# 32-head self-attention on one core: the batch loop written out, values and row sums in one product, one inversion for two tiles, sums added on GpSimd, the output product split over two steps

## What is computed

```python
q, k, v = split(x @ Wqkv)                 # 32 query heads of 16, 8 key heads of 16, 8 value heads of 16
s = causal(q_h @ k_g.T * 16 ** -0.5)      # 256 x 256 for each of 32 heads
p = exp(s - rowmax(s)); o_h = (p @ v_g) / rowsum(p)
o = o_even - lam * o_odd                  # differential attention, lam from four vectors
y = (o * (1 - LAMBDA_INIT)) @ w @ Wproj   # done as two products, output_1 and output_2
out = layernorm(x + y)
```

## Time and profile before

| | |
|---|---|
| median of 3 runs | 2690.73 us (2687.52 to 2690.77) |
| profiled execution | 2702.13 us, span 2700.4 us |
| busy in the span | PE 2359.3 us, DVE 1950.1, ACT 1423.8, POOL 1619.5 |
| self-attention stage | the first 680 us of the span |
| `self_neg_max`, two maxima a slot, L1503 and L1504 | 256 each, 422 and 682 ns |
| exponentials of the stage, L1366 | 256, 813 ns |
| masks of the stage, L1582 | 256, 659 ns |

### The profile page before, as it was taken

How to read it: one execution, slowest core, us unless ns; L and a number is a source line. 1 busy time by engine, 2 the same in 40 slices (tenths; PEclk the granted TensorE clock), 3 DMA queues, 4 the chain that set the end, 5 groups by cost and what they waited for, 6 DMA issues and landing times. The chain is left out here.

```text
span 2700.4 us, 64172 instructions
## 1 busy us (share of the span) xinstructions
PE 2359.3 (87%) x23480; PEld 1977.8 (73%) x23480; DVE 1950.1 (72%) x3223; ACT 1423.8 (53%) x2223; POOL 1619.5 (60%) x1937
## 2 busy tenths in 40 slices
PE   5999999998698986988999984888995899987998
PEld 5777777776566656988999983777775667656998
DVE  3677776776488973536888866999984488875776
ACT  2566656665366653324556654566562466653333
POOL 3677666764467752175666656777664488863443
PEclk9899999999699987999999997999996799988999
DMA  8566565651798951135666653011001888841111
GB/s 206 132 154 163 144 140 144 159 129 33 215 223 220 230 131 36 41 114 194 224 219 222 226 173 112 28 44 48 21 13 56 222 211 224 215 119 41 49 57 51
DMA packets 227284, 363.44 MB, mean 135 GB/s; under 512 B 51968, under 2 KB 156416, under 8 KB 219520
## 3 DMA queue, kind: packets, MB, share of 16 engines
q1 hardware_dynamic: 207392, 281.32, 39.3%
q0 software_dynamic: 17376, 78.13, 8.5%
q10 hardware_dynamic: 2304, 1.05, 0.2%
HBM read 231.72 MB, written 133.69 MB: 135 GB/s over the span
## 5 line engine op out<-in xcount | busy, mean ns | idle before, releaser
L1366 ACT ACTIVATE self_probs<-self_score_ps 128x768 f32<-128x768 f32 x256 | 208.2, 813 | 199.2 <-PE self_score_ps L1268 197.3
L1582 POOL TENSOR_SCALAR_AFFINE_SELECT self_probs<-self_probs 128x512 f32<-128x512 f32 x256 | 168.5, 659 | 174.5 <-ACT self_probs L1366 174.5
L1503 DVE TENSOR_REDUCE self_neg_max<-self_max_ps 128x2 f32<-128x256 f32 x256 | 108.1, 422 | 178.5 <-PE self_max_ps L88 178.5
L647 ACT ACTIVATE cross_probs<-cross_score_ps 128x1024 f32<-128x1024 f32 x128 | 131.2, 1025 | 101.6 <-PE cross_score_ps L545 100.1
L745 DVE TENSOR_REDUCE cross_neg_max<-cross_max_ps 128x4 f32<-128x1024 f32 x128 | 154.7, 1212 | 39.9 <-PE cross_max_ps L524 39.8
L1504 DVE TENSOR_REDUCE self_neg_max<-self_max_ps 128x2 f32<-128x512 f32 x256 | 174.5, 682 | 0.0
L2294 POOL TENSOR_TENSOR moee_h_lo<-moee_h,moee_h_hi 128x512 fp32r<-128x512 f32 x78 | 112.5, 1443 | 92.1 <-ACT moee_h_hi L2031 91.3
L739 DVE TENSOR_REDUCE causal_block_max<-causal_max_ps 128x6 f32<-128x768 f32 x128 | 120.9, 946 | 56.1 <-PE causal_max_ps L88 55.6
L3589 POOL TENSOR_TENSOR ffn_g_lo<-ffn_g_full,ffn_g_hi 128x512 fp32r<-128x512 f32 x64 | 82.2, 1284 | 129.5 <-ACT ffn_g_hi L3475 116.5
L2031 ACT ACTIVATE moee_h_hi<-moee_h 128x512 fp32r<-128x512 f32 x110 | 69.6, 633 | 167.6 <-DVE moee_h L2197 159.4
L647 ACT ACTIVATE causal_probs<-causal_score_ps 128x768 f32<-128x768 f32 x128 | 103.6, 810 | 98.9 <-PE causal_score_ps L545 98.8
(11 more groups left out here) (507 smaller groups left out, 9493.7 us busy)
## 6 DMA issues: line engine op xcount, KB each, us to landing
self_q<-self_q_split SPq DMA_DIRECT2D x48, 512.0 KB, 3.6
self_q_raw<-self_q SPq DMA_DIRECT2D x32, 768.0 KB, 8.1
cross_stacks<-cross_qk SPq DMA_DIRECT2D x64, 384.0 KB, 6.5
causal_stacks<-causal_qk SPq DMA_DIRECT2D x64, 384.0 KB, 6.5
moe_y_tiles<-lasting_y_out SPq DMA_DIRECT2D x55, 256.0 KB
mid<-lasting_y_out SPq DMA_DIRECT2D x48, 256.0 KB, 2.2
x_tiles<-zeros SPq DMA_DIRECT2D x16, 624.0 KB, 5.0
moee_xT<-x_tiles SPq DMA_DIRECT2D x39, 256.0 KB
```

Of the source, the lines that this page charges most:

```text
L647: nc.scalar.activation(probs[i // 2][:, a, :, lo:], score_ps[:, :, lo:], ACT.Exp, scale=HD ** -0.5).then_inc(prob_ready, 1)
L1366: nc.scalar.activation(probs[g % 4][:, a, :, P:], score_ps[:, :, P:], ACT.Exp, scale=HD ** -0.5).then_inc(prob_ready, 1)
L1503: dve.tensor_reduce(neg_max[:, tile, :, c, 0:1], bank[:, :, 0:P], AX.X, ALU.max, negate=True)
L1582: pool.affine_select(diagonal, diagonal, [[0, 2], [0, 2], [1, P]], ALU.is_ge, zero, base=0, channel_multiplier=-1).then_inc(prob_masked, 1)
```

## The change

`run` writes out all twenty steps; the hardware loop of the stage is gone. `weighted` has 8 products where it had 16: `v_pad` holds a column of ones in the unused half, and each group writes its own half of `out_ps`. ScalarE makes a masked copy with the halves exchanged (`cross_weighted`), VectorE adds the rest (`merge`), and this frees the bank. GpSimd adds the sums of two tiles (`add_sums`) and VectorE inverts once for two tiles; a shuffle spreads the inverse (`scale`). The two maxima of a slot become one over three blocks and a join for each tile.

Work is moved as well: `transpose_x`, `x_hi` and `x_lo` of a batch from slot 0 of a step to slots 12 and 13 of the step before; `output_1` from slots 12 and 14 to 14 and slot 0 of the next step; `y_hi` and `y_lo` to slots 0 and 1; `part_o` to slots 6, 7, 14 and 15; `finish_rows` from slot 7 to 11; ScalarE's `sort_q` is cut in halves, in slots 3, 4, 12 and 13. The transfer of `ones` is gone, for all stages.

```diff
 def mask_half(pe, bank, identb, mask, ab, step):
-    diagonal = bank.rearrange("p (j t) -> p j t", t=P)[:, 0::3, first:]
+    diagonal = bank[:, 0:3 * P].rearrange("p (j t) -> p j t", t=P)[:, 0::2, first:]
...
-        run = lambda eng, body: batches(eng, body, -3, B, 6, 5)
+        def run(eng, body):
+            for t in range(-3, B + 1):
+                body(Step(0, t))
...
             def output_1(st, half):
-                if not st.has(-1):
+                if half == 0 and not st.has(-1):
                     pe.wait_ge(w_lo_ready, 2)
                 if half == 0:
-                    if st.has(3):
+                    if st.has(4):
+                        pe.wait_ge(xlo_ready, st.done(4))
+                    elif st.has(3):
                         pe.wait_ge(v_kept, st.done(3))
                     elif st.has(-1):
                         pe.wait_ge(r_ready, st.done(-1))
-                n = st.at(0) * TILES + 2 * half + 2
+                n = st.at(-half) * TILES + 2 * half + 2
                 pe.wait_ge(ohi_ready, n)
                 pe.wait_ge(olo_ready, n)
...
                 if par == 0 and (tile or st.has(d - 1)):
-                    pe.wait_ge(comb_ready, st.at(d) * TILES + tile)
-                for part in range(4):
-                    k = part % 2
-
+                    pe.wait_ge(merged_ready, st.at(d) * TILES + tile)
+                for k in range(QT):
                     first_q = P if k == 1 else 0
                     cols = slice((1 - k) * S + first_q, (2 - k) * S)
                     for quad in range(4):
                         rows = slice(32 * quad, 32 * quad + 32)
-                        if part < 2:
-                            lhs = v_pad[p][:, 2 * (4 * (quad // 2) + tile) + k, par, :, :].rearrange("p a e -> p (a e)")
-                            out0 = 0
-                        else:
-                            lhs, out0 = ones[:, par, :], S
-                        last = pe.matmul(out_ps[rows, out0 + first_q:out0 + S], lhs,
+                        lhs = v_pad[p][:, 2 * (4 * (quad // 2) + tile) + k, par, :, :].rearrange("p a e -> p (a e)")
+                        last = pe.matmul(out_ps[rows, par * S + first_q:(par + 1) * S], lhs,
                                          probs[g % 4][:, quad % 2, quad // 2, cols],
-                                         start=(par == 0 and part == 0),
-                                         stop=(par == 1 and part == 3), skip_group_check=True)
+                                         start=k == 0, stop=k == QT - 1, skip_group_check=True)
...
+            def join_max(st, tile):
+                dve.wait_ge(max_kept, st.at(1) * PAIRS + 4 * tile + 4)
+                if st.has(0):
                     dve.wait_ge(maxT_done, st.at(0) * TILES + tile + 1)
+                dve.tensor_tensor(neg_max[:, tile], block_max[:, :, :, 0:2], block_max[:, :, :, 0::2],
+                                  ALU.min).then_inc(max_joined, 1)
+
+            def merge(st, d, tile):
+
+                n, b = st.at(d) * TILES + tile, tile % 2
+                dve.wait_ge(crossed_ready, n + 1)
+                if tile >= 2 or st.has(d - 1):
+                    dve.wait_ge(o_ready, n - 1)
+                dve.scalar_tensor_tensor(merged[b][:], out_ps[:].rearrange("p (a s) -> p a s", s=S),
+                                         halves[:, 0:1], crossed[b][:], ALU.mult, ALU.add).then_inc(merged_ready, 1)
+
+            def invert(st, d, half):
+                dve.wait_ge(sums_ready, st.at(d) * 2 + half + 1)
+                dve.reciprocal(inv_sum, sums).then_inc(inv_ready, 1)
+
             def normalize(st, d, tile):
 
                 n, b = st.at(d) * TILES + tile, tile % 2
-                dve.wait_ge(comb_ready, n + 1)
-                dve.reciprocal(inv_sum[:, b, :], comb[b][:, 1, :]).then_inc(inv_ready, 1)
-                dve.wait_ge(inv_ready, n + 1)
+                dve.wait_ge(inv_ready, st.at(d) * 2 + tile // 2 + 1)
+                if tile or st.has(d - 1):
+                    dve.wait_ge(o_ready, n)
+                dve.stream_shuffle(scale[:], inv_sum, [HD + b] * HD + [b] * HD).then_inc(scale_ready, 1)
+                dve.wait_ge(scale_ready, n + 1)
                 if tile >= 2 or st.has(d - 1):
                     dve.wait_ge(olo_ready, n - 1)
-                dve.tensor_tensor(o_full[:, b, :], comb[b][:, 0, :], inv_sum[:, b, :],
+                dve.tensor_tensor(o_full[:, b, :], merged[b][:, 0, :], scale[:],
                                   ALU.mult).then_inc(o_ready, 1)
...
+            def add_sums(st, d, half):
+                n = st.at(d) * 2 + half
+                pool.wait_ge(merged_ready, 2 * n + 2)
+                pool.tensor_tensor(sums, merged[0][:, 1, :], merged[1][:, 1, :], ALU.add).then_inc(sums_ready, 1)
```

173 lines of the change are left out of this document (99 added, 74 removed).

## The result

The changed kernel took 2715.06 us, median of four runs (2708.81 to 2722.76). The kernel before took 2689.63 in the same comparison. The ratio is 1.010, with a 95% interval of 1.0075 to 1.0126: 1.0% slower, where the prediction said 1.3% faster. The profiled execution took 2722.76 us, with a span of 2721.0.

A forecast was written before the change was run, and what follows sets the result against it. TensorE was taken to bound a full step, VectorE next. Savings of 15.3 + 3 + 7.6 + 4.5 + 2 - 2 gave 30 us, taken as 34 for overlapping waits: 2656 us, range 2620 to 2684.

The forecast's parts named there:

- The loop: Self stage: writing out steps 3 to 10 removes three back edges, which cost 15.3 us together.
- A group: Products with values and sums on TensorE: each group shrinks from 1.43 us to 0.79, eight groups a step, 5.1 us.
- The wait in slot 7: TensorE waits about 1.8 us a step for VectorE's merge of tile 2 before writing `out_ps` for tile 3.
- The wait in slot 14: TensorE's first output product waits for VectorE's `x_lo`: 1.9 to 3.4 us, taken as 2.7.
- The wait in slot 0: TensorE's second output product waits 0.8 us for `o_lo` of tile 3, made by GpSimd in slot 15.
- the lock: Slot 13: if GpSimd's `sort_k` starts first, VectorE's product with the scale stands until it ends; slot 14 then waits 3.4 us.
- the sum of a full step: Self stage: 31.1 us of TensorE work plus waits of 1.8, 2.7, 0.8 and 0.3 gives 36.7, as before.
- Steps 13 and 14 are set by VectorE: End of the self stage: VectorE's 26.93 us, about 1.5 and its own waits make 30; 3.8 us saved each.
- The head: Start of the self stage: step 0 saves 4.5 us, step -1 saves 2, eight more memsets cost 0.5.
- TensorE alone decides: Rival: waits of slots 7, 14 and 0 are hidden, full step 31.1 us, kernel 2594 us; chance 0.10.
- The lock strikes in every step: Rival: slot 14 costs 3.4 us each time, 8 us more in all, 2665 us; chance 0.18.
- the lock and a clock that falls: Rival: after slot 14's 3.4 us wait TensorE runs slow, 2 us more a step, 2688 us, no change; chance 0.14.

The follow-up runs named there:

- the loop alone: The kernel before with only the self stage's hardware loop written out: 0.9956 of before, 12 us less.
- the wait filled: The changed kernel with 44 unneeded products of 128 bf16 columns on TensorE in slot 14's wait, ahead of the first output product: 1.0037 of before.
- the kernel with the sort in slot 12: The changed kernel with GpSimd's sorting of k moved from slot 13 to slot 12: 1.0002 of before.
- The kernel without the sums: The kernel before with the loop written out and the products with `ones` left out for all batches but the first: 0.9843 of before.
- the kernel with ten products in slot 7: The changed kernel with `x_lo` made before slot 13's normalize, k's sort in slot 12, ten unneeded products ahead of slot 7's merge wait: 0.9918 of before.
- `x_lo` first: The changed kernel with VectorE making `x_lo` ahead of the normalizing product in slot 13: 0.9982 of before.
- two products to a slot: The changed kernel with `x_lo` before slot 13's normalize, k's sort in slot 12, two unneeded products in every slot of steps 13 and 14: 0.9969 of before.

## Why the prediction was wrong

The account of the self stage, in us against the kernel before, from the traces (where a step starts, and where the last product of the stage does; by another row as the start of a step the parts shift by up to 0.4):

| part | forecast | measured | missed by |
|---|---|---|---|
| head and steps -1, 0 | -6 | +0.9 | 7 |
| steps 1 to 11, and the loop's edges | -15.3 | 26.9 - 15.3 = +11.6 | 27 |
| step 12 | -3 | -1.5 | 1.5 |
| steps 13 and 14 | -7.6 | +13.0 | 21 |
| step 15 and the tail | +1.5 | +6.3 | 5 |
| sum | -30 | +30 | 61 |

The terms of the prediction add up to 30, and it then took 34 for small waits that overlap. The measured column is 30.3, and the profiled execution is 20.6 us above that of before; the other 10 came back between the experts and the causal stage, which the change leaves alone. The time from the first `moee_y_ps` to the first product of the causal stage is 1040 us in the trace of before, 1030 in that of after, and 1023 to 1047 in those of the experiments, so I put it down to no cause.

**What held.** The loop: 15.3 forecast, 14.5 in the trace of the loop alone. A group: 0.79 us. The wait in slot 7: 1.8 forecast; 0.98 for the merge and 0.43 for the maxima in a full step, 1.83 in steps 13 and 14. The wait in slot 14: 2.7 taken of 1.9 to 3.4; it is 2.67, and 0.59 for the exponential ahead of it, near the upper end. The wait in slot 0: 0.8 forecast, at most 0.7. The walk over VectorE's slots was sound, and so was the lock: the page "SBUF — State Buffer" of the Trainium skill, section "SBUF: two separate sides", says that whichever of the two engines starts first holds it, and the sort does so in every step. TensorE's work in a full step was put at 31.1 and is 31.6 (34.27 with the wait filled, less 2.63 for the 44 products), VectorE's at about 30 and is 29.9.

**The step that failed** is the sum of a full step: "31.1 + 1.8 + 2.7 + 0.8 + 0.3 = 36.7". It adds waits as if TensorE came out of them as fast as it went in, and so puts the clock's term at nothing. At the full clock the step would be 37.3, as the filled wait shows, 0.6 above the forecast; the clock makes it 38.7, and 39.2 on average over the eleven, since the low stretch is longer in some (a step of 44.1 us among them). The row for it was in hand: an edge of the loop cost 5.1 us where the wait was 3.16. Busy time by stretch of the kernel before, behind the three edges, has the clock too:

```profile
276.90:280.10 3.20, 3.20 (x42) 1.77 (x38) 1.78 (x4) 1.04 (x2) 3.12 (x5) 0.50 0.57 136
355.40:358.60 3.20, 3.20 (x38) 1.64 (x36) 1.62 (x3) 0.74 (x2) 3.11 (x4) 0.50 0.77 166
430.50:437.10 6.60, 5.83 (x49) 4.03 (x53) 2.58 (x5) 2.49 (x4) 3.07 (x5) 0.50 0.20 41
```

The prediction used the row only for a rival, at 2 us a step, which is the right size, and gave it 0.14, because the wait was to be 2.7 and not 3.4. A wait of 2.67 us is long enough, and one of 1.3 still brings it in ten steps of eleven (the kernel with the sort in slot 12).

**The second failure** is "Steps 13 and 14 are set by VectorE ... 30". That took the saved TensorE work of steps that have no projections as a gain. The trace of before warned of it, if less plainly: TensorE was idle for 2.5 of 33.77 us there already, where a full step had 0.5. With the groups' 5.1 us gone as well, the granted clock is 0.74. The kernel without the sums loses 5.4 of the 13.0 us, so that much comes with the shrunken groups alone; no run parts the other 7.6 among the new and moved operations. Nor was 30 us reached where the clock came back. The nearest row is step 14 of the kernel with ten products in slot 7, which takes 34.1 us at a clock of 0.95, against 39.8 at 0.70 in the changed kernel. By it some 6 us a step are the clock's, and some 4 are waits that the 30 left out (an estimate from these two rows).

**The head** was missed by 7 us. Step 0 was to take 32.3 (36.76 less 4.5), and took 39.6 at a clock of 0.77. With `x_lo` first it took 31.4 at 1.00. Busy time by stretch of step 0, changed kernel and `x_lo` first:

```profile
86.21:125.81 39.60, 36.10 (x386) 26.41 (x382) 26.91 (x38) 23.63 (x36) 24.30 (x32) 0.77 0.58 138
```

```profile
86.11:117.50 31.39, 28.34 (x387) 21.05 (x384) 25.58 (x38) 23.23 (x36) 24.76 (x33) 1.00 0.70 173
```

Here too the clock is the term that the sum lacked. What decides it at this place isn't shown: in the other kernels that come from the changed one, step 0 takes between 31.1 and 39.5 us.

**The rivals.** "TensorE alone decides" is refuted: VectorE's waits are real. "The lock strikes in every step" and "the lock and a clock that falls" both came true; the second one's price of 2688 left out the last steps, the head and the tail, where TensorE waits 5.22 us for `o_lo` instead of 2.83, with the low clock before and behind; the 1.50 for `y_lo` were 1.51 before. TensorE in order of time in the tail of the changed kernel:

```profile
697.20 0.55 PE L79 MATMUL self_misc<-self_wo_hi,self_o_hi 128*128 128x256 f32 x1 [5.22 <-POOL self_o_lo L1643]
...
701.61 0.55 PE L79 MATMUL self_misc<-self_wo_hi,self_y_hi 128*128 128x256 f32 x1 [1.50 <-DVE self_y_lo L1603]
```

**What stays open.** What brings the clock back, and so why in steps 13 and 14 it stays low for 20 us of dense work and in most full steps for less than 7. Why two products to a slot made these steps worse (48.0 and 46.0 us) than none. Why ten in slot 7 kept the clock for most of step 14 and not in step 13, and whether a wait there that is really filled would do so in both. Which of the new operations makes the other 7.6 us of steps 13 and 14. Whether the loop, put back into the changed kernel, would cost its 15 us there too, was not tried.

## What to carry to other kernels

Where TensorE runs at its full clock with almost no idle time, its work is also what holds the clock: price a new wait with the slow stretch behind it (here 1.3 to 2 us for a wait of 2.7), and read the granted clock of the stretch behind the waits that the kernel already has. Before taking work off TensorE, ask which engine's queue is the next in line and how late it already is at each place where TensorE meets it; here 5.1 us less work gave 2.3. If a wait can't be taken away, move the instruction that is waited for ahead of its neighbours in its queue, and the neighbour that holds it up to another slot; products that nobody needs, put into the wait itself, are a stopgap, but look at the trace whether they start when the wait does, and whether the clock is better: spread over the slots they made two steps longer.

## What the runs showed of the hardware

- A wait of 2.7 us in a stream of otherwise dense products brought a granted clock of 0.50 in each of the eleven full steps, for 5.84 us of work in the step shown. Filled with 44 products of 128 columns it stayed at 1.00 in all but one. The Trainium skill, page "TensorE: Matmul & The Clock Gate", section "HAM oscillation — how this bites in real kernels", tells of the same with waits of about 3 to 5 us for DMA between short pieces of work. The trace agrees in kind, here with a shorter wait for VectorE in each step.
- A wait of 1.3 us brought it in ten of eleven full steps; the one without took 35.31 us, its neighbours 37.12 and 37.34.
- Useless products made the kernel 0.6% faster in one place and 0.4% slower in another: 0.9926 became 0.9969 with two a slot.
- A sorting copy of 1.94 us on GpSimd held VectorE's product of two SBUF operands at 1.91 us instead of 0.42. Whether the product started 0.31, 0.55 or about 0.9 us behind the sort, it ended 0.28 or 0.29 behind it; with the sort a slot earlier and `x_lo` ahead of the product, none was longer than 0.78 us from 100 to 580 us.
- A product of 128 bf16 columns at the full clock cost 0.073 us each in a row of six (0.44 a slot), 0.060 in a row of 44 (2.63 us).
